# A three-layer graph network on one core: comparisons, counts, variance and the output stage moved between slots and engines

## What is computed

```python
def _sage_conv(h, src, dst, Wl, bl, Wr):
    msg = h[src]
    s = jax.ops.segment_sum(msg, dst, num_segments=N_NODES)
    cnt = jax.ops.segment_sum(jnp.ones((src.shape[0], 1), h.dtype), dst, num_segments=N_NODES)
    agg = s / jnp.maximum(cnt, 1.0)
    return agg @ Wl.T + bl + h @ Wr.T

h, residual = x, 0.0
for Wl, bl, Wr, g, b in params:          # three layers
    h = residual + _sage_conv(h, src, dst, Wl, bl, Wr)
    h = _layer_norm(h, g, b)             # (h - mean) * rsqrt(var + 1e-5) * g + b
    h = _prelu(h, a_prelu)
    residual = h
return _layernorm(x + h)
```

## Time and profile before

| | us |
|---|---|
| median of 3 runs | 2248.23 |
| the profiled execution | 2247.24 |
| its span, first to last instruction | 2245.4 |
| TensorE busy | 2059.0 (92%) |
| VectorE busy | 1747.1 (78%) |
| GpSimd busy | 1442.3 (64%) |
| ScalarE busy | 1101.8 (49%) |
| mean granted clock of TensorE | 0.972 |

### The profile page before, as it was taken

One profiled execution on the slowest core, in us unless ns is written; L12 is line 12 of the kernel. 1 busy time (PEld: TensorE's weight loads), 2 busy tenths in 40 slices (PEclk: granted clock), 3 DMA queues, 4 the chain that ended last, 5 costly groups with the idle time before them and its releaser, 6 DMA issues.

```text
span 2245.4 us, 30803 instructions
## 1 busy us (share of the span) xinstructions
PE 2059.0 (92%) x10342; PEld 1704.5 (76%) x10342; DVE 1747.1 (78%) x2971; ACT 1101.8 (49%) x2169; POOL 1442.3 (64%) x1198
## 2 busy tenths in 40 slices
PE   6768988999999999999999999999899999999991
PEld 4557877777878888788888888887688888888880
DVE  7659788778887778877777777788877777777773
ACT  3324344344333345344333333457677666676664
POOL 2885667766676645544444444358877777778776
PEclk8989999999999999999999999999999999999996
DMA  5345656655566544444444444354555655556642
GB/s 178 135 140 192 213 194 191 201 197 184 191 198 198 192 158 169 160 141 144 149 150 147 143 141 141 123 192 173 194 187 191 189 190 189 197 192 186 193 157 101
DMA packets 180940, 387.45 MB, mean 173 GB/s; under 512 B 20107, under 2 KB 20552, under 8 KB 180782
## 3 DMA queue, kind: packets, MB, share of 16 engines
q1 hardware_dynamic: 142222, 271.80, 36.6%
q0 software_dynamic: 38560, 113.67, 15.8%
HBM read 220.81 MB, written 164.79 MB: 172 GB/s over the span
## 4 chain that ended last, share of the span: by engine, by line
PE 54%; DVE 12%; issue 6%; POOL 3%; ACT 2%; ACTq 0%; POOLq 0%; DVEq 0%
PE ps_z L372 44%; PE ps_s L365 5%; PE ps_t L353 4%; DVE same L765 3%; DVE y L749 2%; ACT hT_hi L473 2%; DVE hT_lo L726 2%; POOL out L637 2%; DVE ps_z L736 2%; DVE over L763 1%; DVE o_sb L796 1%; PE ps_z L390 1%; DVE hout L754 1%; POOL y L620 1%; POOL orstd L626 1%
## 5 line engine op out<-in xcount | busy, mean ns | idle before, releaser
L372 PE MATMUL ps_z<-w_hi,hT_hi 128*128 128x512 f32 x1884 | 761.7, 404 | 1.4 <-DVE y L749 1.4
L620 POOL TENSOR_TENSOR y<-y,shift 128x1024 f32<-128x1024 f32 (+1 forms) x237 | 585.4, 2470 | 252.0 <-DVE y L749 249.8
L372 PE MATMUL ps_z<-w_hi,hT_lo 128*128 128x512 f32 x1884 | 744.2, 395 | 0.0
L372 PE MATMUL ps_z<-w_lo,hT_hi 128*128 128x512 f32 x1884 | 743.9, 395 | 0.0
L485 ACT ACTIVATE junk<-ps_z 128x512 f32<-128x512 f32 x471 | 280.8, 596 | 927.7 <-DVE ps_z L736 786.0
L372 PEld LDWEIGHTS ps_z<-w_hi,hT_lo 128*128 128x128 f32 x1884 | 356.3, 189 | 80.7
L372 PEld LDWEIGHTS ps_z<-w_lo,hT_hi 128*128 128x128 f32 x1884 | 358.1, 190 | 73.9
L372 PEld LDWEIGHTS ps_z<-w_hi,hT_hi 128*128 128x128 f32 x1884 | 359.3, 191 | 71.3 <-DVE y L749 1.9
L614 POOL TENSOR_TENSOR rstd<-veps,minus_half 128x2 f32<-128x2 f32 (+1 forms) x237 | 170.7, 720 | 355.8 <-DVE veps L741 353.7
L736 DVE TENSOR_TENSOR ps_z<-ps_z,bias_rows 128x512 f32<-128x512 f32 x314 | 215.9, 693 | 229.5 <-PE ps_z L372 228.3
L749 DVE SCALAR_TENSOR_TENSOR y<-ps_z,rstd,gain 128x512 f32<-128x512 f32 x471 | 329.7, 740 | 64.0 <-POOL rstd L614 64.0
(11 more groups left out here) (126 smaller groups left out, 2386.3 us busy)
## 6 DMA issues: line engine op xcount, KB each, us to landing
h_scratch<-hout SPq DMA_DIRECT2D x156, 512.0 KB, 3.0
hin<-h_scratch SPq DMA_DIRECT2D x156, 512.0 KB, 4.4
x_by_slot<-hin SPq DMA_DIRECT2D x78, 512.0 KB, 3.2
o_sb<-x_by_slot SPq DMA_DIRECT2D x78, 512.0 KB, 3.7
rowtab<-edge_row_table SPq DMA_DIRECT2D x60, 256.0 KB, 4.4
stage<-in_WrT SPq DMA_DIRECT2D x3, 1024.0 KB, 7.9
stage<-in_WlT SPq DMA_DIRECT2D x3, 1024.0 KB, 6.2
hin<-in_x,node_get POOLq DMA_INDIRECT x157, 3.5
```

The source lines that it names most:

```text
L372: mm = pe.matmul(acc, a[:, k, :], ww[:, k, :], start=start, stop=stop and k == KC - 1 and a is a_lo)
L620: nc.gpsimd.tensor_tensor(y[u.r2][:, 0:u.n, :], y[u.r2][:, 0:u.n, :], moved, ALU.add).then_inc(shifted, 1)
```

## The change

- `compare` runs three units ahead and directly behind `normal`; `load_rowtab` is five ahead.
- The splits of the second count begin one slot earlier (`COUNT_SLOT` 0), and the counting matmuls stand one slot behind them, between `turn` and the messages.
- `variance` and `out_variance` go from VectorE to ScalarE, as an Identity activation with scale 1/D and a bias tile `eps`. `normal` waits for the `prelu` of unit u - 2 by a semaphore.
- `out_norm` and `put_out` are five units behind instead of six and seven; `out_norm` stands ahead of `part`, and `out_root` (four behind) at the end of GpSimd's slot. The ring has 6 buffers.
- Weight 1 is loaded inside SyncE's loop, at T = -1, behind the first `turn`.

```diff
-        OB = 8
+        OB = 6
...
-        COUNT_SLOT = 1
+        COUNT_SLOT = 0
         COUNTS_A_SLOT = 3
-        TABLE_SLOT = COUNT_SLOT + -(-ET // COUNTS_A_SLOT)
+        TABLE_SLOT = COUNT_SLOT + 1 + -(-ET // COUNTS_A_SLOT)
...
             def load_weight(w):
+                if w == 1:
+                    sp.wait_ge(turned, 1)
...
-            load_weight(1)
...
-            for T in range(-4, UNITS + 3):
-                for stage_, ahead in ((store_x, 2), (load_h, 3), (load_residual, -1), (load_rowtab, 4), (store_h, -3)):
+            for T in range(-5, UNITS + 3):
+                for stage_, ahead in ((store_x, 2), (load_h, 3), (load_residual, -1), (load_rowtab, 5), (store_h, -3)):
...
                 for w, at in W_SLOT.items():
-                    if w > 1 and T == at - 4:
+                    if T == at - 4:
                         load_weight(w)
...
                 if ahead.exists:
                     turn(ahead)
+                for i in range(ET):
+                    if T == COUNT_SLOT + 1 + i // COUNTS_A_SLOT:
+                        if i == 0:
+                            pe.wait_ge(table_done, 1)
+                        count_tile(ET + i)
+                if ahead.exists:
                     sum_messages(ahead, 0)
...
-                for i in range(ET):
-                    if T == COUNT_SLOT + i // COUNTS_A_SLOT:
-                        if i == 0:
-                            pe.wait_ge(table_done, 1)
-                        count_tile(ET + i)
...
+            def variance(u):
+                act.wait_ge(squared, u.upto)
+                reach(act, rstd_done, u.no - 1)
+                nc.scalar.activation(veps[u.r2][:, 0:u.n], ssq[u.r2][:, 0:u.n], ACT.Identity, scale=1.0 / D,
+                                     bias=eps[:, 0:1]).then_inc(veps_done, 1)
...
+            def out_variance(u):
+                if u.l < L - 1:
+                    return
+                act.wait_ge(o_squared, u.o_upto)
+                nc.scalar.activation(oveps[u.ring][:, 0:u.n], ossq[u.ring][:, 0:u.n], ACT.Identity, scale=1.0 / D,
+                                     bias=eps[:, 0:1]).then_inc(o_veps, 1)
...
-            for T in range(-1, UNITS + 6):
+            for T in range(-1, UNITS + 5):
                 last, ahead, u = Unit(T - 1), Unit(T + 1), Unit(T)
                 if last.exists:
                     square(last, 1)
+                    variance(last)
                 if ahead.exists:
                     take_high(ahead)
+                old = Unit(T - 5)
+                if old.exists:
+                    out_norm(old, 0)
+                    out_norm(old, 1)
                 old = Unit(T - 2)
                 if old.exists:
                     part(old)
-                old = Unit(T - 6)
-                if old.exists:
-                    out_norm(old, 0)
-                    out_norm(old, 1)
                 old = Unit(T - 4)
                 if old.exists:
                     out_mean(old)
                     out_square(old, 0)
                     out_square(old, 1)
+                    out_variance(old)
...
-            for T in range(-3, UNITS + 8):
+            for T in range(-3, UNITS + 6):
                 last = Unit(T - 1)
                 if last.exists:
                     root(last)
-                old = Unit(T - 5)
-                if old.exists:
-                    out_root(old)
...
                 if last.exists:
                     add_shift(last)
-                old = Unit(T - 7)
+                old = Unit(T - 5)
                 if old.exists:
                     put_out(old)
+                old = Unit(T - 4)
+                if old.exists:
+                    out_root(old)
...
             def normal(u):
                 dve.wait_ge(rstd_done, u.no + 1)
+                reach(dve, h_done, u.no - 1)
...
-                if last.exists:
-                    variance(last)
-                if Unit(T - 5).exists:
-                    out_variance(Unit(T - 5))
...
                 if last.exists:
                     normal(last)
+                if Unit(T + 3).exists:
+                    compare(Unit(T + 3))
...
                 if u.exists:
                     add_bias(u, 0)
-                if Unit(T + 2).exists:
-                    compare(Unit(T + 2))
```

More of the change, by code:

```diff
@@ L107, in build_program @@
         minus_half = sb("minus_half", [P, 2])
+        eps = sb("eps", [P, 1])
         hin = [sb(f"hin{i}", [P, 2, D]) for i in range(3)]
@@ L736, in add_bias @@
                 nc.vector.tensor_tensor(acc, acc, bias_rows[:, u.l, :], ALU.add).then_inc(biased, 1)
-            def variance(u):
-                dve.wait_ge(squared, u.upto)
-                reach(dve, rstd_done, u.no - 1)
-                nc.vector.tensor_scalar(veps[u.r2][:, 0:u.n], ssq[u.r2][:, 0:u.n], 1.0 / D, EPS,
-                                        ALU.mult, ALU.add).then_inc(veps_done, 1)
             def normal(u):
                 dve.wait_ge(rstd_done, u.no + 1)
+                reach(dve, h_done, u.no - 1)
                 if u.no == 0:
@@ L797, in out_sum @@
                                                    ALU.mult, ALU.add, accum_out=osum[u.ring][:, j:j + 1]).then_inc(o_summed, 1)
-            def out_variance(u):
-                if u.l < L - 1:
-                    return
-                dve.wait_ge(o_squared, u.o_upto)
-                nc.vector.tensor_scalar(oveps[u.ring][:, 0:u.n], ossq[u.ring][:, 0:u.n], 1.0 / D, EPS,
-                                        ALU.mult, ALU.add).then_inc(o_veps, 1)
             nc.vector.memset(ones_short[:], 1.0)
@@ L809, in vector_program @@
             nc.vector.memset(minus_half[:], -0.5)
+            nc.vector.memset(eps[:], EPS)
             nc.vector.memset(bias_full[:].bitcast(F32), 0.0)
@@ L879, in vector_program @@
             dve.wait_ge(bias_done, 1)
-            for T in range(-1, UNITS + 6):
+            for T in range(-1, UNITS + 3):
                 last, ahead, u = Unit(T - 1), Unit(T + 1), Unit(T)
```

## The result

The changed kernel takes 2180.28 us (median of 4 runs, 2179.82 to 2182.75) against 2248.72 for the kernel before: a ratio of 0.9706, with a 95% interval of 0.9693 to 0.9718. The forecast was 2161, with a range from 2136 to 2192. So it is faster, inside the range, and 19 us slower than the point; the forecast's own range, that of rival A, ended at 2176. The profiled execution took 2179.82 us, of which the span is 2178.05.

A forecast was written before the change was run, and what follows sets the result against it. TensorE, busy 92% of the span, was taken to bound the kernel, its largest wait being for `same`. Terms summed to -87.2 us from 2247.24, giving 2160.0, and 2161 for the median; range 2136 to 2192.

The forecast's parts named there:

- rival A: The forecast itself: waits for `same` gone, layer 2 paced by GpSimd's longer frame; 2161 us, own range 2148 to 2176; chance 0.52.
- layer 0, edge part: Layer 0's 20 cycles: earlier comparison regains the 51.8 us lost, 3.0 given back for small waits; -48.8.
- layer 1, edge part: Layer 1's edge part: 542.71 us falls to its gapless 519.3 through the earlier comparison; -23.4, bounds 20 and 23.4.
- counts, weight 1, start: Early slots: counting matmuls one slot later gain 2 us, weight 1 loaded inside the loop gains 1.1.
- layer 2, T = 158 to 174: Layer 2's plain part: seven slots of 8.32 us and one of 6.86 become eight of 9.3; +9.3, bounds -10 and +13.
- layer 2, edge part: Layer 2's 19 steady cycles: 28.84 us falls to 28.5, set by GpSimd's frames; -6.3, bounds -18.2 and +19.
- tail: After TensorE's end: two fewer late frames give -8 us, four longer ones take back 4; -4, bounds -8 and +2.
- rival C: Layer 2: ScalarE and GpSimd wait for each other in turn, cycle 29.8 us; 2190 us; chance 0.19.
- the forecast's hold of 2.4: VectorE, edge units: every moved comparison is held some 2.4 us by GpSimd's shift addition, covered by the long slot.
- GpSimd has no slack: Layer 2, old output order: GpSimd's next `rstd` comes 8.33 us after the last, equal to the slot of 8.32.
- rival B: Layer 2 is free as well, GpSimd's frame near 8.4 us and TensorE binding; 31 less, 2130 us; chance 0.17.
- D: Slower than before: rival C's ring closes within fewer frames, layer 2 cycle at 34 us, 2265 us; chance 0.04.

The follow-up runs named there:

- run 7: Changed kernel with `eps` allotted last and the output's steps in their old order with 8 buffers: 2142.99 us, ratio 0.9549.
- run 3: Changed kernel with `eps` allotted behind all tiles that stay, layer 0's weights keeping their address: 2168.30 us.
- run 1: Kernel before with an unused 32-byte tile ahead of `hin`, moving the activations and all that follows: 2257.64 us, ratio 1.0056.
- experiment 5: Two runs: changed kernel, only layer 0's weights moved 160 bytes up, 2173.85 us; kernel before, everything moved 32 bytes together, 2245.23 us.

## Why the prediction was right, and where it was not

Measured between the two profiled executions, by the prediction's own steps:

| step | forecast | measured |
|---|---|---|
| layer 0, edge part | -48.8 | -50.2 |
| layer 1, edge part | -23.4 | -13.2 |
| layer 1, plain part, and the slots around the edge parts | -1.7 | +3.1 |
| counts, weight 1, start | -3.1 | -2.9 |
| layer 2, T = 158 to 174 | +9.3 | +13.2 |
| slot ahead of layer 2's first edge unit | -9.2 | -8.6 |
| layer 2, edge part | -6.3 | -10.2 |
| from there to TensorE's end | 0 | +1.9 |
| tail | -4 | -0.5 |
| sum | -87.2 | -67.4 |

The total lies in the stated range, but outside the forecast's own range of 2148 to 2176. The stated range holds it because it took in rival C, which did not occur; in that the prediction was lucky.

**Layer 0: right, by two parts.** I gave the gain to the comparison and called the variance a thing that TensorE hides. The comparison alone gives 36.0 (587.2 to 551.2), the variance the rest: without it, layer 0 is 15.8 us longer. (On ScalarE it takes 0.30 us, where I had put the 0.189 of `oneg`.) VectorE's groups of `over` and `same` show the hold of the earlier trace rows in numbers, in the kernel before, the changed one, and run 7 (busy us, mean ns):

```profile
L763 DVE SCALAR_TENSOR_TENSOR over<-rowtab,dlast 128x128 f32<-128x128 f32 x120 | 111.1, 926 | 0.0
L765 DVE SCALAR_TENSOR_TENSOR same<-rowtab,dcol 128x128 f32<-128x128 f32 x120 | 88.9, 741 | 0.0
```

```profile
L778 DVE SCALAR_TENSOR_TENSOR same<-rowtab,dcol 128x128 f32<-128x128 f32 x120 | 88.2, 735 | 0.0
L776 DVE SCALAR_TENSOR_TENSOR over<-rowtab,dlast 128x128 f32<-128x128 f32 x120 | 43.7, 364 | 0.0
```

```profile
L778 DVE SCALAR_TENSOR_TENSOR same<-rowtab,dcol 128x128 f32<-128x128 f32 x120 | 43.3, 361 | 0.0
L776 DVE SCALAR_TENSOR_TENSOR over<-rowtab,dlast 128x128 f32<-128x128 f32 x120 | 41.0, 341 | 0.0
```

Free, each takes 0.34. I had expected a hold in every edge unit. In layer 0 there is none and in layer 1 one; in layer 2 of the changed kernel there is one in each of the 20 edge units, which is why the mean of `same` stayed at 735. With the old output order (run 7) layer 2 has none either. One of the 20, on VectorE and then on GpSimd:

```profile
1798.25 2.66 DVE L778 SCALAR_TENSOR_TENSOR same<-rowtab,dcol 128x128 f32<-128x128 f32 x1
```

```profile
1798.34 2.42 POOL L638 TENSOR_TENSOR y<-y,shift 128x1024 f32<-128x1024 f32 x1
```

It ends just behind the shift addition, and TensorE has no gap in that cycle (28.21 busy of 28.21): there the forecast's hold of 2.4 came, and was covered. In an edge unit of layer 0, GpSimd's message gathers stand between the normalization (ended at 436.66) and the shift addition (begun at 440.56), and the four comparisons were over by 437.71. VectorE there:

```profile
435.27 1.39 DVE L762 SCALAR_TENSOR_TENSOR y<-ps_z,rstd,gain 128x512 f32<-128x512 f32 x2
436.58 0.34 DVE L776 SCALAR_TENSOR_TENSOR over<-rowtab,dlast 128x128 f32<-128x128 f32 x1
436.84 0.34 DVE L778 SCALAR_TENSOR_TENSOR same<-rowtab,dcol 128x128 f32<-128x128 f32 x1
...
437.37 0.34 DVE L778 SCALAR_TENSOR_TENSOR same<-rowtab,dcol 128x128 f32<-128x128 f32 x1
...
440.52 3.56 DVE L767 SCALAR_TENSOR_TENSOR hout<-hout,slope_less,y 128x1024 f32<-128x1024 f32 x1
```

The port rule that I cited from the Trainium skill ("SBUF — State Buffer", Who interferes with whom) is about two instructions that overlap in time; in layer 0 the queue order kept them apart, in layer 2 it didn't, and both agree with the rule. What is held in layer 0 now is PReLU, 3.56 us beside that addition, and TensorE has no gap there.

**Layer 1: the step that failed.** "Layer 1's should take 519.3 by its own gapless slots" took for granted that a gapless slot is a constant of the work. The waits went entirely, but the edge part took 529.53, 10.2 more than that sum. With `eps` last (run 3) it takes 523.37, so 6.2 come from the 32 bytes that `eps` put between weights and activations. With the ring of 8 as well (run 7) it takes 521.01, so another 2.4, taken in this order, come from the ring of 6, which moved the sums by 384 bytes. The last 1.7 is in the sum itself: a gapless slot ahead of an edge unit takes 8.15 to 8.18, not 6.33 + 1.77. The plain part lost 2.0, of which 1.9 is in its matmuls, as in run 1. Some 1 us around these parts stays with `eps` last too, and no run explains it. Both diff lines, `eps` and `OB = 6`, I had priced at nothing, and the -23.4, with bounds of 20 and 23.4, came out at -13.2. The Trainium skill, "SBUF — State Buffer", Operand start alignment, says that a start at a multiple of the element size is allowed everywhere, and adds "This is about legality, not speed". Layer 1 agrees in so far as an allowed start was slower, at 6.47 against 6.35 us; what counted was the distance of two starts (experiment 5), on which that section says nothing.

**The start of layer 1.** The 1.7 of the earlier normalization did not come: TensorE waits 1.6 us for `y` there, and waited 1.4 before.

**Layer 2: the mechanism was right, two sizes were off.** GpSimd's instructions over one plain frame of the changed kernel:

```profile
1493.90 0.74 POOL L644 TENSOR_TENSOR orstd<-oveps,minus_half 128x2 f32<-128x2 f32 x1
1494.72 0.69 POOL L647 TENSOR_TENSOR omove<-oneg,orstd 128x2 f32<-128x2 f32 x1
1495.37 0.69 POOL L632 TENSOR_TENSOR rstd<-veps,minus_half 128x2 f32<-128x2 f32 x1
1497.59 2.37 POOL L638 TENSOR_TENSOR y<-y,shift 128x1024 f32<-128x1024 f32 x1 [1.52 <-DVE y L762]
1500.13 1.82 POOL L655 DMA_INDIRECT out<-o_sb,node_put  x1 [0.17 <-issue]
1502.25 0.97 POOL L655 DMA_INDIRECT out<-o_sb,node_put  x1 [0.30 <-issue]
...
1504.76 0.68 POOL L632 TENSOR_TENSOR rstd<-veps,minus_half 128x2 f32<-128x2 f32 x1
```

From `rstd` to `rstd` 9.39, where the forecast had 9.3, and the empty 1.52 that it named. The parts differ: the shift addition is no longer held (2.37, not 3.38), the first scatter is longer (1.82) and `omove` takes 0.69. These errors nearly cancelled, by luck. The plain part cost 3.9 more than forecast because TensorE fell to this pace earlier: T = 158 to 166 already give 3.4, before the eight slots that I had counted.

For the steady cycles I took 28.5; it is 28.2. The step behind it, "GpSimd has no slack" in the old order, held in the plain part only (65.5 us for eight slots with the comparison alone too). In the edge cycles the 28.84 was VectorE's queue, with a held comparison: with that moved, GpSimd does 27.88 in the old order. So in the edge part of a kernel with the old order TensorE binds, as rival B had it, and in the plain part GpSimd does in either order: B's 31 us were too many, the order is worth some 14. Rivals C and D did not occur: ScalarE does wait 175.7 us for `omove`, the sign that I had named, but the cycle is 28.2 and not 29.8, without a gap on TensorE.

**Tail.** Two frames fewer, as forecast, but the late ones grew from 4.0 to some 5.1 us, for the scatter now waits for ScalarE's norm, which waits for the `omove` just issued:

```profile
2148.76 0.75 POOL L644 TENSOR_TENSOR orstd<-oveps,minus_half 128x2 f32<-128x2 f32 x1
2149.58 0.19 POOL L647 TENSOR_TENSOR omove<-oneg,orstd 128x2 f32<-128x2 f32 x1
2151.43 1.03 POOL L655 DMA_INDIRECT out<-o_sb,node_put  x1 [1.65 <-ACT o_sb L543]
...
2153.91 0.72 POOL L644 TENSOR_TENSOR orstd<-oveps,minus_half 128x2 f32<-128x2 f32 x1 [0.17 <-ACT oveps L536]
```

**Left open.** Weight 1's load was not tried by itself, nor which of the three moves of the output's order costs the 14; the argument from GpSimd's frame names `out_root`, last in it, and it is only argued.

## What to carry to other kernels

Count the gain of a removed wait against the slots' gapless length, and then compare that length in both traces too: if busy time per instruction has changed, no wait will explain it. A new small tile, or a ring with fewer buffers, is an edit of its own, so allot it behind the tiles that TensorE reads, or print the distances. And when a change has several parts, run the first alone: here one part gave 3.5%, all of them 2.9%, and all but the output's order, with the addresses set right, 4.8%.

## What the hardware showed that I had not expected

The pace of a stream of 128x512 matmuls depended on where its operands lie relative to each other. A plain slot took 6.33 to 6.37 us with the stationary tile's start a multiple of 256 bytes from the moving tile's and 6.46 to 6.49 at 32, 64, 128 or 160 bytes more, at a granted clock of 1.00 and with no wait; moving both together changed nothing (2245.23 against 2244.89). Other distances were not tried for the activations. The weight load overlaps the running matmul here, 5.33 us of a slot of 6.46. The Trainium skill, "TensorE: Matmul & The Clock Gate", Step-by-step: what each phase is for, says that loading the next stationary tile takes no SBUF read bandwidth from the running matmul. From that alone I would not have expected the distance to matter, and here it did; whether the effect lies in that load, no run shows. On 2180 us the move of `eps` is worth 12 to 22, of the size of a well-chosen change.
